# A macaron transformer block on one core: a separate first gate that loads its input transposed as well, splits weights in place, routes in two batches and starts the first row fetches itself

## What is computed

```python
x = x + 0.5 * _L0_ffn_ref(_layernorm(x), gate_weight, gate_up_proj, down_proj, similarity_matrix)
x = x + _L0_attn_ref(_layernorm(x), Wq_down, ..., Wc)
x = x + 0.5 * _L0_ffn_ref(_layernorm(x), gate_weight, gate_up_proj, down_proj, similarity_matrix)
```

```python
probs = softmax(x @ gate_weight.T)                 # N x 8
top_w, top_i = top_k(probs, 2)                     # two experts for each token, weights normalised
primary_mask[top_i[:, :1]] = True                  # experts that are some token's first choice
expert_map = where(~primary_mask & (best_sim >= 0.7), best_j, ids)
gu = einsum('nh,efh->enf', x, gate_up_proj)
y = einsum('enf,ehf->enh', silu(g) * u, down_proj)
out = einsum('ne,enh->nh', combine, y)
```

## Time and profile before

| | us |
|---|---|
| median of 3 runs | 1285.59 |
| lowest, highest run | 1278.75, 1290.84 |
| the profiled execution: time, span | 1279.61, 1277.8 |
| first gate, from the span's start to DVE's last instruction | 98.25 |
| from there to the first matmul of the experts | 8.73 |
| first experts, until POOL's last scatter is issued | 192.89 |

### The profile page before, as it was taken

The page is one execution under the profiler, slowest core; times in us unless marked ns, Lnnn a source line. Parts: engine busy times, 40 slices in busy tenths (PEclk is TensorE's granted clock), DMA queues, the critical chain, the costliest instruction groups (busy, mean ns, idle before and its releaser), DMA issues. The chain is left out here.

```text
span 1277.8 us, 25859 instructions
## 1 busy us (share of the span) xinstructions
PE 1033.2 (81%) x9306; PEld 729.1 (57%) x9306; DVE 816.5 (64%) x1701; ACT 704.5 (55%) x1570; POOL 538.6 (42%) x713
## 2 busy tenths in 40 slices
PE   7426999997899599999999999996385159999940
PEld 3115888886788445555555555553362148888830
DVE  5793444442776378888888888881267954444428
ACT  7713554542675137777777777775157335555520
POOL 3604777774565302122242232232106237777720
PEclk9667999996799759999999999998597579999975
DMA  8606333333485623334543643531127013333339
GB/s 258 203 1 200 103 104 103 101 104 124 145 257 173 172 46 93 76 93 95 123 96 79 131 100 95 111 77 47 49 82 233 17 42 103 104 104 104 99 125 311
DMA packets 95737, 149.67 MB, mean 117 GB/s; under 512 B 15744, under 2 KB 65664, under 8 KB 95616
## 3 DMA queue, kind: packets, MB, share of 16 engines
q1 hardware_dynamic: 81792, 110.25, 31.2%
q0 software_dynamic: 13824, 37.77, 9.1%
HBM read 90.81 MB, written 56.89 MB: 116 GB/s over the span
## 5 line engine op out<-in xcount | busy, mean ns | idle before, releaser
L1440 ACT ACTIVATE spare<-h_psS 128x512 f32<-128x512 f32 x576 | 313.0, 598 | 94.9 <-PE h_psS L1365 78.4
L1468 DVE TENSOR_REDUCE h_part<-h_psM 128x2 f32<-128x1024 f32 (+3 forms) x256 | 258.2, 1023 | 29.2 <-PE h_psM L1344 18.4
L1504 POOL TENSOR_SCALAR_AFFINE_SELECT spare<-spare 128x256 f32<-128x256 f32 x256 | 99.8, 408 | 316.4 <-ACT spare L1440 316.4
L561 PE MATMUL m_psG<-m_wgu,m_x_hi 128*128 x576 | 195.8, 421 | 0.5 <-DVE m_x_lo L635 0.4
L1392 PE MATMUL h_psO<-spare,a_VP 128*17 128x256 f32 (+3 forms) x3072 | 188.5, 333 | 9.4 <-ACT h_OT L1431 8.8
L533 POOL DMA_INDIRECT m_xg<-xn,m_slot_u x144 | 139.8, 971 | 118.1 <-SPq L521 34.6
L1344 PE MATMUL h_psM<-h_KT,h_QT 48*128 48x512 f32 (+3 forms) x768 | 167.0, 452 | 16.7 <-DMA h_QT<-a_QD 13.1
L539 POOL DMA_INDIRECT ys<-m_y,m_slot_u x144 | 142.4, 989 | 65.3 <-issue 35.4
L645 DVE TENSOR_TENSOR m_h<-m_act_g,m_psG 128x256 f32<-128x256 f32 x144 | 60.6, 421 | 136.0 <-ACT m_act_g L619 132.3
L1365 PE MATMUL h_psS<-h_QT,h_KT 49*128 49x512 f32 (+3 forms) x768 | 142.8, 379 | 0.0
L1344 PEld LDWEIGHTS h_psM<-h_KT,h_QT 48*128 48x128 f32 x768 | 76.0, 193 | 105.3 <-issue 85.7
(11 more groups left out here) (208 smaller groups left out, 1712.0 us busy)
## 6 DMA issues: line engine op xcount, KB each, us to landing
spare<-gate_up SPq DMA_DIRECT2D x16, 512.0 KB, 4.0
xn<-spare SPq DMA_DIRECT2D x16, 512.0 KB, 5.1
p_yg<-ys SPq DMA_DIRECT2D x16, 512.0 KB, 5.8
a_KD<-spare SPq DMA_DIRECT2D x32, 256.0 KB, 3.0
h_KT<-a_KD SPq DMA_DIRECT2D x64, 128.0 KB
h_QT<-a_QD SPq DMA_DIRECT2D x64, 128.0 KB
a_OD<-h_OT SPq DMA_DIRECT2D x128, 64.0 KB, 2.4
m_yg<-ys SPq DMA_DIRECT2D x16, 512.0 KB, 6.8
```

Source lines behind the costliest of these rows:

```text
L561: m = pe.matmul(out, s[:, c, :], ww[:, bass.ds(at + c * width, width)], start=(n == 0), stop=(n == 3 * CC - 1))
L1440: act.activation(prob[k % NP][:, h, :], psS[x % NS][:, :], ACT.Exp).then_inc(s_read, 1)
L1468: m = dve.tensor_reduce(out, psM[k % NM][:, :, at:at + n], AX.X, ALU.max, negate=True)
L1504: m = pool.affine_select(block, block, [[0, 2], [1, P]], ALU.is_ge, 0.0, 0, -1)
```

## The change

The first mixture of experts gets a gate function of its own, `first_gate`; the second keeps `gate`. The host also passes the input transposed (`x_turned`, 256 x 4096, 4 MB). In `first_gate`:

- PE no longer turns the input and ACT no longer evacuates it (L194 and L279 have no counterpart): each piece is also loaded from `x_turned` into one of four buffers in `spare`, in 256 rows of 2 KB.
- An expert's weights are loaded straight to where their low part will stand; ACT writes the high part beside it and the low part is written over the raw values. No load waits for the split. POOL writes the low parts of experts 0 to 5, DVE those of 6 and 7 at the very end.
- Routing has two batches of 16 tiles. The routing code moved into a class `Route` with the same instructions, twice as wide in tiles (`choices` and `place` 2 times instead of 4). Root and inverse are taken twice, of 16 tiles each.
- ACT's order is written out piece by piece. DVE normalises pieces 6 and 7 (`normal`, one tensor_scalar 128 x 256 a tile).
- SP alternates x and x_turned pieces with the weights of experts 0 to 3, then stores and the other weights.
- DVE writes the row column of `slot_u` first (`slots_done`), and POOL issues the four first gathers still in the gate block, while DVE goes on with the block list, weights and low parts. The buffers xg are allocated before the gate.
- `early.load` waits: its three weights are issued after h of 4, 8 and 12 blocks, the rest after 16.

```diff
+    W, RA, RB, RT = 4, 3, 1, 4
+    NH = NT // W
+
+    BY_ACT, BY_DVE = tuple(range(NH - 2)), (NH - 2, NH - 1)
+
+    BY_POOL = 6
...
+            def _(sp):
+                def weights(e):
+                    sp.dma_start(wgu[1][:, e * ng:(e + 1) * ng].bitcast(F32).rearrange("p (c f) -> p c f", c=CC),
+                                 gu_d[e, :, :].rearrange("(c p) f -> p c f", p=P)).then_inc(w_in[e], 16)
+                    sp.dma_start(wdn[1][:, e * nd:(e + 1) * nd].bitcast(F32).rearrange("p (c f) -> p c f", c=CC),
+                                 dn_d[e, :, :].rearrange("(c p) f -> p c f", p=P)).then_inc(w_in[e], 16)
...
+                def turned(h):
+                    if h >= RT:
+                        sp.wait_ge(scored, h - RT + 1)
+                    sp.dma_start(xT[h % RT][:, :, :], xt_t[:, :, W * P * h:W * P * (h + 1)]).then_inc(t_in[h], 16)
...
+                for h in range(NH):
+                    load(h)
+                    turned(h)
+                    if h % 2 == 1:
+                        weights(h // 2)
+                store(0)
+                store(1)
+                route.similarities(sp, sim_d)
+                weights(4)
+                store(2)
+                weights(5)
+                store(6)
+                store(3)
+                weights(6)
+                store(4)
+                weights(7)
+                store(5)
+                store(7)
...
+            def _(pe):
+                def score(h):
+                    pe.wait_ge(t_in[h], 16)
+                    if h >= 2:
+                        pe.wait_ge(lgt_done, h - 1)
+                    for c in range(CC):
+                        m = pe.matmul(psL[h % 2][0:E, :], middle[:, c, :], xT[h % RT][:, c, :], start=c == 0, stop=c == CC - 1)
+                    m.then_inc(scored, 1)
...
+                for h in range(NH):
+                    score(h)
+                    if h >= 1:
+                        back(h - 1)
+                    if h == NH - 2:
+                        route.ranks(pe, 0)
+                back(NH - 1)
+                route.ranks(pe, 1)
+                route.products(pe)
...
+                for h in range(4):
+                    across(h)
+                high(0)
+                across(4)
+                deviate(0)
+                normal(0)
+                across(5)
+                high(1)
+                normal(1)
+                across(6)
+                across(7)
+                high(2)
+                deviate(1)
+                normal(2)
+                high(3)
+                normal(3)
+                high(4)
+                normal(4)
+                normal(5)
+                route.exponentials(act)
+                high(5)
+                for i in range(route.CH):
+                    route.partitions(act, i)
+                for e in range(BY_POOL, E):
+                    high(e)
...
+                for e in range(BY_POOL):
+                    for n, (h, l) in enumerate(parts(e)):
+                        pool.wait_ge(whi_done, 3 * e + n + 1)
+                        pool.tensor_tensor(l, l.bitcast(F32), h.bitcast(F32), ALU.subtract).then_inc(wlo_done, 1)
+                pool.wait_ge(wlo_done, 3 * BY_POOL)
+                pool.wait_ge(route.slots_done, 1)
+                for j in range(RA):
+                    pool.wait_ge(xa_out[j], 16 * len(BY_ACT[j::RA]))
+                for j in range(RB):
+                    pool.wait_ge(xb_out[j], 16 * len(BY_DVE[j::RB]))
+                for b, rows in enumerate(xg):
+                    pool.indirect_dma_start(rows[:, :], None, xn_d[:, :],
+                                            bass.IndirectOffsetOnAxis(ap=slot_u[:, b, 0:1], axis=0)).then_inc(gathered[b], 16)
...
+                def choices(q):
+                    dve.wait_ge(lg_done, route.FROM[q + 1] // W)
+                    route.choices(dve, T, q, logits[q][:, 0:route.size(q) * E].rearrange("p (t e) -> p t e", e=E))
...
+                for h in range(5):
+                    measure(h)
+                choices(0)
+                invert(0)
+                for h in range(5, NH):
+                    measure(h)
+                route.place(dve, T, 0)
+                choices(1)
+                invert(1)
+                normal(BY_DVE[0])
+                route.open_gap(dve, T, rstd[:, :])
+                route.low_places(dve, 0)
+                route.begins(dve, T)
+                route.place(dve, T, 1)
+                route.shift(dve, T)
+                for i in range(3):
+                    route.block_places(dve, i)
+                normal(BY_DVE[1])
+                route.low_places(dve, 1)
+                for i in range(3, route.CH):
+                    route.block_places(dve, i)
+                route.similar(dve, T)
+                route.slots(dve, T)
+                route.experts(dve, T)
+                route.weights(dve, T)
+                for e in range(BY_POOL, E):
+                    for n, (h, l) in enumerate(parts(e)):
+                        dve.wait_ge(whi_done, 3 * e + n + 1)
+                        dve.tensor_tensor(l, l.bitcast(F32), h.bitcast(F32), ALU.subtract).then_inc(low_done, 1)
...
+        xg = [sb(f"xg{j}", [P, C]) for j in range(R)]
...
-                        early.load(sp)
+                        early.load(sp, h_done)
...
-                    for b in range(R):
+                    for b in range(0 if x_d is None else R, R):
                         gather(b)
...
-    def load(self, sp):
+    def load(self, sp, passed):
         DH = self.sh.DH
-        for w in (1, 0, 2):
+        for n, w in enumerate((1, 0, 2)):
+            sp.wait_ge(passed, 4 * n + 4)
             sp.dma_start(self.down[w][:, :, :], self.w_d[w].rearrange("(r p) c -> p r c", p=P)).then_inc(self.down_in[w], 16)
+        sp.wait_ge(passed, 16)
```

350 lines of the change are left out of this document (343 added, 7 removed).

## The result

The changed kernel takes 1274.05 us (median of 10 runs, 1269.7 to 1281.2), the kernel before 1289.6 (median of 10 on the same chip). The ratio is 0.989, with a 95% interval of 0.986 to 0.992: 10 to 18 us less, with 13.8 in the middle (the two medians themselves lie 15.6 apart). I had said 1272 us, and a gain of 12.5 us on the profiled execution of before.

The account below looks back on a forecast made before the run. The gate's chain up to PE's first turn, ACT then DVE, was taken as bound: 13.5 us gained less 1.0 for spaced loads takes 1279.6 to 1267.1, plus 6.0 for the median 1273.1; said 1272, range 1262 to 1284.

Parts of the forecast that it names:

- Part 1, input: Gate's input loads: once hidden, they now set the pace, with piece 4 in at 25.7 us and piece 7 at 36.5.
- the right end of the bounds: Turned input's strided reads: full rate of 365 GB/s taken, two thirds of it (+5 us) as the other end.
- My 9 us by the Trainium skill: Turned input's 4.19 MB: at the skill's 207 GB/s 20.3 instead of 11.5 us, almost 9 later; not in the sum.
- Part 2, first half: Gate up to the second choices: choices(0) 4.5 us, ending 33.8; ACT's rows make PE wait; place(0) on DVE ends at 42.7.
- Part 3, tail: DVE from the end of the last choices to the list: 28.8 us before POOL's disturbance; list complete at 83.2.
- the disturbance by POOL: DVE's routing slowed by POOL's splits of experts 2 to 5: 7.2 us taken, low 4, high 11.
- Part 4, fetches and border: Gate's end: fetches cost nothing, six low parts 3.7 us, border 1.0; first turn at 93.5 us, gain 13.5.
- Part 5, spaced loads: First experts: each of four spaced attention loads delays PE by 0 to 3 us, 0.25 taken, 1 us in all.
- the sign would have turned: First experts: a delay of 3.4 us a load or more decides the sign of the whole change.
- a sign of being wrong: First experts: PE waiting for xg behind blocks 4, 8, 12 and 16, or experts needing more than 193 us.
- Rival (c): First experts: spaced loads stall PE, 11 us at one stall a load (1283) or 22 at two (1295); chance 0.10.
- The sum: Whole kernel: 13.5 us gained at the first turn less 1.0 for spaced loads, 12.5 us less than 1279.6.

Follow-up runs that it names:

- e7: Changed kernel with attention loads in 256 KB pieces, weights of experts 2 and 3 behind all input, scores taken earlier; 1353.0 us on a slower chip.
- e3: Changed kernel without POOL's low parts of experts 2 to 5 (result not the reference's); three runs 1264.2 to 1266.9 us, three 1272.8 to 1275.1.
- e5: Changed kernel with the first four fetches back behind the border, at the start of the experts; median 1279.0 us, ratio 0.996 to the kernel before.
- e1: Changed kernel with the attention's loads issued at once at the start of the experts instead of spaced; median 1273.6 us, ratio 0.992 to the kernel before.
- e10: The changed kernel unaltered, run again on a chip where both kernels are some 6% slower; median 1350.8 us, ratio 0.987 to the kernel before.

## Why the prediction was right, step by step

**Part 1, input.** I had piece 4 at 25.7 us and piece 7 at 36.5; PE began them at 24.43 and 37.01. Piece 7 says little, since it did not wait for its load. Piece 6 did: the same sum (9.70 MB up to its end) gives 33.6, and PE began it at 33.16. Full rate was the right end of the bounds: in windows between 20 and 35 us the DMAs moved 363 to 381 GB/s, and the reads of 2 KB pieces at a distance of 16 KB cost nothing that shows. My 9 us by the Trainium skill (DMA: Bandwidth & Descriptors, Latency and other measured facts) had no ground: its 207 GB/s at 512 KiB is the rate of copies between two DRAM tensors, for which it gives 214 as full rate, and not a loss to be set against 365. e7 confirms the mechanism, with piece 6 sooner by 2.0 us for the 0.79 MB that were taken out ahead of it.

**Part 2, first half.** Choices(0) 4.57 us long (4.5 said), ending 32.86 (33.8 said). The second choices started at 40.95 (42.7). PE's wait for ACT was there in its place (1.06 us ahead of its last turns, which end at 40.85), but DVE did not wait behind it, for its own place(0) ended at 40.86. POOL disturbed place(0) by 1.0 only, and the scores behind piece 4 ran at full clock.

**Part 3, tail.** Without POOL it is 29.6 us from the end of the second choices to the list (e3: 44.99 to 74.58; 28.8 said). The four `normal` on DVE took 1.37 us, 0.34 each (0.35 said). The mis-sized term is the disturbance by POOL: 7.2 taken, 10 measured (upper bound 11). The rows gave 2 to 3 us an expert, which for four is 8 to 12; I had taken less, as if part of it would miss DVE's chain, and none did. By place it was 5.1 in the choices (3.0 said) and about 5 behind them (4.2 said). List at 84.97 instead of 83.2: 2.9 late by POOL, 0.8 by the tail, 1.75 early by the start.

**Part 4, fetches and border.** Six low parts took 3.7 us as said. The border cost 0.33 instead of 1.0, since no fetch stands behind it. First turn 94.57 against 93.5 said; the gain at this mark 12.4 instead of 13.5. e5 splits the 8.73 us of old gap nearly as I had: 4.7 for the loads that no longer meet the fetch (I had written 4.3, though my rows give 8.73 - 4.06 = 4.7), 3.7 for the fetch in the gate.

**Part 5, spaced loads.** This is the step that was wrong in size: 0.25 us a load taken, 1.06 measured (4.25 in four), against 3.4 from which the sign would have turned. What I had called a sign of being wrong came true: PE waited behind the loads, and the experts needed 197.96 us, more than the 193 that I had named. Rival (c) was the right mechanism at a smaller price. The changed kernel's timeline of SP, POOL and PE answers to the earlier trace rows:

```profile
117.76 0.37 SPq L1271 DMA_DIRECT2D spare<-wq_down  x1
...
119.79 0.97 POOL L1047 DMA_INDIRECT m_xg<-xn,m_slot_u  x1 [0.31 <-PE m_psX L1083]
...
125.69 0.44 PE L1083 MATMUL m_psX<-ident,m_xg 128*128 128x128 f32 x2 [0.57 <-DMA m_xg<-xn,m_slot_u]
```

A fetch issued 2 us after the load was used at 125.69, 4.9 us after its issue ended, 3.1 more than the 1.8 of an undisturbed one; and 1 MB at 365 GB/s is 2.9 us. The load's own traffic is seen in windows of 1 us (columns: length, clock, DMA share, GB/s):

```profile
119.00:120.00 1.00, 1.00 0.56 112
120.00:121.00 1.00, 1.00 0.97 329
...
123.00:124.00 1.00, 1.00 0.92 343
124.00:125.00 1.00, 1.00 0.48 135
```

It fills the DMAs from about 120 to 124 us, and the list of issues has this load landing 5.9 us after its issue, so at about 124. The fetch's issue ended at 120.76, as that traffic began, and its rows were used some 1.7 us after the load had landed. So it stood behind the whole load. The room was 1.8 us, so it was 1.3 late, and one block later PE lost 0.9 again. I had looked only at the fetch ahead, which was half landed when the load began, and not at the next one, issued behind it. The Trainium skill (DMA: Bandwidth & Descriptors, Queues, rings and completion order) says that a DMA engine takes turns between its queues by packet. By that a fetch beside a load should have been late by well under 1 us; the fetch at 119.79 does not bear it out here.

**The sum.** By marks, 12.4 gained less 4.2 lost beside the loads is 8 us, where I had 12.5: both of my errors, 1.1 at the first turn and 3.2 beside the loads, made the gain too large. The runs say 13.8 (10 to 18). So the median came out right partly by luck: what my sum had too much was made up by some 6 us that no mark accounts for. The profiled run of before, on which I had built, was nearly its fastest; its mean granted clock was 0.887, while the 23 runs of before beside e1 to e5 have 0.871 to 0.886 and their times rise as the clock falls (1281 us at 0.882, 1290 at 0.876, 1296 at 0.871). Eight of the ten runs of the changed kernel have 0.886 to 0.893, but on the chip of those 23 its stand-in e1 has 0.873 to 0.888, hardly more than before. The windows of e3 show one place where some 9 us are lost so, the first part of the heads. Whether the change makes that rarer, or which of its marks does, stays open: there is no trace of before at the lower clock.

## What to carry to other kernels

A transfer that shares the DMAs with a just-in-time fetch is judged by the size of one piece against the fetch's room, not by how far apart the pieces are: four loads of 1 MB cost PE 4.2 us both at once and spaced, sixteen of 256 KB cost 0.2 (both on chips where the blocks ran at 2.56 us; on the slower ones no gain was seen, and halves of 512 KB settled nothing). Before work is handed from VectorE to GpSimd, ask what runs on VectorE at that time: here each expert's split cost VectorE 2.5 us on the other engine and 1.81 on its own. Before a mark of one trace is set against a mark of another, compare traces of the same code: here they lay up to 1.9 us apart. And build a forecast on several runs, since the one with the profile may be the exception.

## What the runs showed of the hardware that I had not expected

- GpSimd's `tensor_tensor` on SBUF does not slow VectorE's instructions with two inputs by a share; it makes them wait: 0.29 us became 1.24, 0.19 became 4.39 behind three instructions in a row, while a reduce kept its 0.28. `tensor_scalar` was slowed too (32 low_places 5.28 to 8.44).
- The same program needed 187.0 us from the first to the last of 72 turns on one chip and 221.7 on another (e10), in a stage with two indirect transfers a block, while its marks in the gate agreed to 0.2 us. Loads in pieces, worth 5 us on the one, showed no gain on the other.
- PE's clock may come back 20 us later at the same place of the same work (53 instead of 34 us into the heads), which moves a whole run by 9 us. It did so in 3 of 14 traces.
- A single score of 1.88 us at full clock took 3.30 at a granted clock of 0.54. The first choices, which wait behind it, started at 28.29 us with the slow score and at 26.83 with the quick one.
